# Score pass of a graph-attention kernel: three of four tiles as three rounded products, masks from ScalarE's signs

## What is computed

```
node_support = adj_n @ h
edge_output  = gru_cell(node_support, h, edge weights)
for each of 3 heads:
    hW = h @ W[k]
    hp = (adj_n > 0) @ hW ;  hm = (adj_n < 0) @ hW
    e_plus  = leaky_relu([hp, hm] @ a[k]) ; e_minus = leaky_relu([hm, hp] @ a[k])
    att = softmax over columns of (e_plus where adj_n > 0, e_minus where adj_n < 0, else -9e15)
    edge_support += (att * adj_n) @ hW / 3
node_output = gru_cell(edge_support, h, node weights)
x + diag(adj) * edge_output + diag(adj) * node_output
```

## Time and profile before

| what | value |
|---|---|
| median of the runs | 2155.43 us |
| the profiled execution | 2154.86 us, span 2153.1 us |
| TensorE busy | 89% of the span |
| VectorE, ScalarE busy | 77%, 58% |
| score pass, first table product to last f32 product | 922.0 to 1236.0 us |
| one of its chunks 1 to 7 | 39.8 us |

### The profile page before, as it was taken

The page is one execution under the profiler, slowest core; times in us unless marked ns, Lnnn a source line. Parts: engine busy times, 40 slices in busy tenths (PEclk is TensorE's granted clock), DMA queues, the critical chain, the costliest instruction groups (busy, mean ns, idle before and its releaser), DMA issues.

```text
span 2153.1 us, 21391 instructions
## 1 busy us (share of the span) xinstructions
PE 1910.1 (89%) x7805; PEld 1162.6 (54%) x7805; DVE 1652.7 (77%) x2442; ACT 1248.5 (58%) x1393; POOL 0.8 (0%) x7
## 2 busy tenths in 40 slices
PE   2336999699988889899999959899999999999997
PEld 1224888478878888844444436544444444444443
DVE  4668999698868989976656553498898888988985
ACT  3445666356669898810000010298878788887873
POOL 0000000000000000000000000000000000000000
PEclk9999999899999999999999979999999999999998
DMA  9999999488866767678998658632342323323220
GB/s 389 429 429 360 338 337 340 178 296 320 321 254 233 254 220 251 226 282 299 322 331 299 238 228 295 206 113 98 118 141 84 126 99 112 111 104 127 101 75 11
DMA packets 81561, 489.48 MB, mean 227 GB/s; under 512 B 8449, under 2 KB 12546, under 8 KB 36402
## 3 DMA queue, kind: packets, MB, share of 16 engines
q1 hardware_dynamic: 77138, 485.94, 61.7%
q10 hardware_dynamic: 4320, 2.20, 0.3%
HBM read 452.36 MB, written 35.75 MB: 227 GB/s over the span
## 4 chain that ended last, share of the span: by engine, by line
PE 70%; DVE 15%; DMA 7%; ACT 6%; issue 2%; SPq 0%; DVEq 0%; ACTq 0%
PE bank L1599 25%; PE bank L1483 10%; DMA ring<-in_adj_rows 6%; PE bank L1411 5%; PE bank L1413 5%; PE bank L1412 5%; PE bank L1561 5%; PE bank L1445 4%; DVE work L1255 3%; ACT work L573 2%; ACT work L566 2%; DVE a_lo L874 2%; PE bank L1478 2%; DVE reg L1255 1%; PE bank L1288 1%
## 5 line engine op out<-in xcount | busy, mean ns | idle before, releaser
L1599 PE MATMUL bank<-work,reg 128*128 128x512 f32 x960 | 423.0, 596 | 17.3 <-DVE ring L1204 11.4
L1255 DVE TENSOR_TENSOR work<-work,ring 128x1536 f32<-128x1536 f32 x160 | 280.2, 1752 | 68.4 <-ACT work L696 67.4
L1599 PEld LDWEIGHTS bank<-work,reg 128*128 128x128 f32 x960 | 182.0, 191 | 246.6 <-issue 220.3
L874 DVE TENSOR_TENSOR a_lo<-ring,a_hi 128x2048 fp32r<-128x2048 f32 x128 | 290.8, 2288 | 31.4 <-ACT a_hi L515 30.5
L515 ACT ACTIVATE a_hi<-ring 128x2048 fp32r<-128x2048 f32 x128 | 244.2, 1913 | 76.4 <-PE bank L1413 76.4
L1445 PE MATMUL bank<-reg,ring 128*128 128x129 f32 x2048 | 244.9, 281 | 36.9 <-DVE ring L988 36.8
L1445 PEld LDWEIGHTS bank<-reg,ring 128*128 128x128 f32 x2048 | 238.7, 197 | 42.4 <-DVE ring L988 32.5
L1599 PE MATMUL bank<-reg 128*128 128x512 f32 x576 | 252.4, 592 | 0.0
L696 ACT ACTIVATE work<-work 128x1536 f32<-128x1536 f32 x160 | 235.3, 1471 | 26.1 <-DVE work L1233 26.1
L1483 PE MATMUL bank<-ring,reg 128*128 128x512 f32 x512 | 236.8, 605 | 0.0
L1411 PE MATMUL bank<-a_hi,s_hi 128*128 128x512 f32 x512 | 207.0, 404 | 21.2 <-DVE a_lo L874 21.2
(11 more groups left out here) (214 smaller groups left out, 2153.5 us busy)
## 6 DMA issues: line engine op xcount, KB each, us to landing
ring<-in_adj_units SPq DMA_DIRECT2D x320, 1024.0 KB, 4.9
ring<-in_adj_rows SPq DMA_DIRECT2D x32, 2048.0 KB, 17.0
masks<-work SPq DMA_DIRECT2D x64, 512.0 KB, 9.0
ring<-masks SPq DMA_DIRECT2D x64, 512.0 KB, 4.5
reg<-lines SPq DMA_DIRECT2D x8, 768.0 KB, 10.1
ring<-lines SPq DMA_DIRECT2D x8, 768.0 KB, 8.0
out<-ring ACTq DMA_DIRECT2D x8, 256.0 KB, 2.3
gru<-in_cells SPq DMA_DIRECT2D x1, 768.0 KB
```

Of the source, the lines that this page charges most:

```text
L874: dve.tensor_tensor(a_lo[:, ring_at(p, g)], ring[:, ring_at(p, g)], a_hi[:, (g % 4) * UNIT:(g % 4 + 1) * UNIT].bitcast(F32), ALU.subtract) ...
L1255: dve.tensor_tensor(tv, tv, spread(ring[:, ring_at("out", g, q * W, W)], HEADS, 1), ALU.mult).then_inc(s_y, 1)
L1599: last = pe.matmul(bank[1 + k][:, :], h, tiles(c * T + t)[:, k * W:(k + 1) * W], start=t == 0, stop=t == T - 1)
```

## The change

In the score pass, of the four tiles of a unit, the first stays one f32 product (`WHOLE` = 1); the other three are made of three fp32r products each. For that ScalarE rounds 128x1536 values of each unit (`high_parts`, three buffers, `HIGHS`) and, in chunk 0, the 128x512 of `h` for that group; VectorE subtracts (`low_parts`). The masks are no longer compared on VectorE from f32 values: ScalarE writes the sign of the whole unit as fp8 (`sign_of`, 128x2048, two buffers in `hT` and `outT`), and VectorE makes the masks from its bits with two int32 operations over 128x512 words. A set mask is now 0.125, and the tables and sums are scaled for it. The steps of a chunk are at other places: on TensorE `turn_edge` behind unit `8c + 1`, `gates` behind `8c + 2`, `turn_cells` behind `8c + 7`; on VectorE and ScalarE as in the diff. Some buffers have moved (`sm_all`, `ucut`, `sums_sb`, the fourth mask buffer).

```diff
+    def sign_of(n):                                   # ScalarE
+        act.wait_ge(*loaded("edge", c, g))
+        if c == g: act.wait_ge(s_fix["edge"], g + 1)
+        if n > 1:  act.wait_ge(s_made, n - 1)
...
+        act.activation(signs[n % 2].bitcast(FP8), ring[:, ring_at("edge", g, c=c)],
+                       ACT.Sign, saturate=False).then_inc(s_sign, 1)
+    def high_parts(n):
...
+        if c == 0:
+            act.wait_ge(s_hkept, g + 1)
+            act.activation(h_hi[:, g * W:(g + 1) * W], reg1[:, g * W:(g + 1) * W], ACT.Copy).then_inc(s_hhi, 1)
+        if n >= HIGHS:
+            act.wait_ge(s_mm["edge"], n - HIGHS + 1)
+        act.activation(edge_hi(n), ring[:, ring_at("edge", g, WHOLE * W, SPLIT, c=c)], ACT.Copy).then_inc(s_ehi, 1)
+    for c in range(C):
+        for g in range(G):
+            n = c * G + g
+            if n == 3:             store_hT(C)
+            if c and g == 2:       keep_edge(c)
+            if c and g == 5:       gates("edge", c)
+            if 2 <= n + 1 < C * G: high_parts(n + 1)
+            if c and g == 6:       candidate("edge", c)
+            if n + 2 < C * G:      sign_of(n + 2)
     def masks(n):                                     # VectorE
         if n >= MASKS:
             dve.wait_ge(s_mm["edge"], n - MASKS + 1)
             dve.wait_ge(s_stored[b], 16 * (n // MASKS))
-        dve.tensor_scalar(made[b][0], src, 0.0, None, ALU.is_gt, saturate=False)
-        dve.tensor_scalar(made[b][1], src, 0.0, None, ALU.is_lt, saturate=False).then_inc(s_mask, 1)
+        dve.wait_ge(s_sign, n + 1)
+        dve.tensor_scalar(minus, code, 2, NONZERO, ALU.logical_shift_right, ALU.bitwise_and).then_inc(s_neg, 1)
+        dve.wait_ge(s_neg, n + 1)
+        dve.scalar_tensor_tensor(plus, code, NONZERO, minus, ALU.bitwise_and, ALU.bitwise_xor).then_inc(s_made, 1)
+    def low_parts(n):
...
+        dve.wait_ge(s_ehi, n + 1)
+        dve.tensor_tensor(a_lo[:, rest], ring[:, rest], edge_hi(n).bitcast(F32), ALU.subtract).then_inc(s_elo, 1)
     for c in range(C):
         for g in range(G):
-            if 4 <= c * G + g + 1 < C * G: masks(c * G + g + 1)
-            if c and g == 0: edge_nodes(c)
-            if c and g == 2: cell_in("edge", c, s)
-            if c and g == 3: cell_end("edge", c, s)
-            if c and g == 5: result("edge", c)
+            if n == 6:             gat_project(C)
+            if c > 1 and g == 2:   result("edge", c - 1)
+            if c and g == 4:       edge_nodes(c)
+            if c and g == 6:       cell_in("edge", c, s)
+            if 2 <= n + 1 < C * G: low_parts(n + 1)
+            if c and g == 7:       cell_end("edge", c, s)
+            if n + 2 < C * G:      masks(n + 2)
+            clear(n + 3)
     def edge_unit(n):                                 # TensorE
         for q in range(Q):
-            last = pe.matmul(nacc, reg1[tile], ring[part])
+            if q < WHOLE: pe.matmul(nacc, reg1[tile], ring[part]); continue
+            if q == WHOLE: pe.wait_ge(s_elo, n + 1)
+            pe.matmul(nacc, h_hi[tile], hi)
+            pe.matmul(nacc, h_hi[tile], a_lo[part])
+            last = pe.matmul(nacc, h_lo[tile], hi)
...
-            if c and g == 0: turn_edge(c)
-            if c and g == 1: gates("edge", c)
-            if c and g == 4: turn_cells("edge", c)
+            if c and g == 1: turn_edge(c)
+            if c and g == 2: gates("edge", c)
+            if c and g == 7: turn_cells("edge", c)
```

More of the change, by code:

```diff
@@ L25 @@
 EPS = 1e-5
+NONZERO = 0x20202020
+MASK_VALUE = 0.125
 SLOPE = 0.2
@@ L188, in gat_acc @@
             return bank[b][:, (i % 2) * 256:(i % 2) * 256 + P + 1]
-        SP = 7168
+        SP = 7680
         sp_all = work[:, SP:SP + T * EPAD // 2].bitcast(BF16)
-        sm_all = work[:, SP + T * EPAD // 2:SP + T * EPAD].bitcast(BF16)
-        ucut = work[:, 6144:6144 + 2 * Q * SCORES]
+        sm_all = reg4[:, N:N + T * EPAD // 2].bitcast(BF16)
+        ucut = gd[:, 0:2 * Q * SCORES]
         def plus_minus(region, b):
@@ L199, in plus_minus, with edge_hi @@
             return both[:, 0:UNIT // 4].bitcast(FP8), both[:, UNIT // 4:UNIT // 2].bitcast(FP8), both.bitcast(FP8)
-        made = [plus_minus(work, b) for b in range(MASKS)]
-        sums_sb = work[:, 4096:4096 + W]
         temps = ring[:, RING_EDGE * UNIT:G * UNIT]
         e_temps = [temps[:, i * W:(i + 1) * W] for i in range(6)]
+        made = [plus_minus(work, b) for b in range(MASKS - 1)] + [plus_minus(temps, 3)]
+        sums_sb = hn[:, :]
+        signs = [b[:, 0:UNIT // 4] for b in (hT, outT)]
+        SPLIT = (Q - WHOLE) * W
+        def edge_hi(n):
+            first = (MASKS - 1) * UNIT // 2 + (n % HIGHS) * SPLIT
+            return a_hi[:, first:first + SPLIT]
         kept = [plus_minus(ring[:, RING_OUT * UNIT:G * UNIT], b) for b in range(MLOADS)]
@@ L606, in candidate @@
                 act.activation(gn, gt, ACT.Tanh).then_inc(s_ga[p], 1)
[L608 to L611, removed]
+            for c in range(C):
+                for g in range(G):
+                    n = c * G + g
+                    if n == 3:
+                        store_hT(C)
+                    if c and g == 2:
+                        keep_edge(c)
+                    if c and g == 5:
+                        gates("edge", c)
+                    if 2 <= n + 1 < C * G:
+                        high_parts(n + 1)
+                    if c and g == 6:
+                        candidate("edge", c)
+                    if n + 2 < C * G:
+                        sign_of(n + 2)
             keep_edge(C)
@@ L997, in clear_diagonal, with clear @@
                 dve.wait_ge(s_fix[p], g + 1)
+            def clear(n):
+                c, g = n // G, n % G
+                if n < C * G and c == g:
+                    dve.wait_ge(*loaded("edge", c, g))
+                    clear_diagonal("edge", g)
             def masks(n):
[L1001 to L1004, removed]
+                b = n % MASKS
                 if n >= MASKS:
@@ L1057, in result @@
                 last.then_inc(s_res[p], 1)
+            clear(0)
             masks(0)
@@ L1062, in _ @@
             gat_nodes_in(C, s)
-            masks(2)
             gat_project(C - 1)
+            low_parts(0)
             gat_nodes_out(C, s)
-            masks(3)
-            gat_project(C)
+            low_parts(1)
             for c in range(C):
@@ L1071, in _ @@
                 for g in range(G):
-                    if 4 <= c * G + g + 1 < C * G:
-                        masks(c * G + g + 1)
-                    if c and g == 0:
+                    n = c * G + g
+                    if n == 6:
+                        gat_project(C)
+                    if c > 1 and g == 2:
+                        result("edge", c - 1)
+                    if c and g == 4:
                         edge_nodes(c)
-                    if c and g == 2:
+                    if c and g == 6:
                         cell_in("edge", c, s)
-                    if c and g == 3:
+                    if 2 <= n + 1 < C * G:
+                        low_parts(n + 1)
+                    if c and g == 7:
                         cell_end("edge", c, s)
-                    if c and g == 5:
-                        result("edge", c)
+                    if n + 2 < C * G:
+                        masks(n + 2)
+                    clear(n + 3)
+            result("edge", C - 1)
             edge_nodes(C)
```

81 lines of the change are left out of this document (64 added, 17 removed).

## The result

The changed kernel took 2171.68 us, the median of four runs (2170.12 to 2172.74), beside 2154.44 us for the kernel before (four runs): a ratio of 1.0079, with a 95% interval of 1.0067 to 1.0091. It is slower, by 17.2 us; 2165 was forecast. The profiled execution took 2170.12 us, with a span of 2168.3.

The account below looks back on a forecast made before the run. TensorE was taken to bound the score pass. Start +5.3, cheaper products -28.8 and seven waits of 4.7 us sum to +9.4 us, so 2165 us from the median of 2155.4; 8-in-10 range 2145 to 2181.

Parts of the forecast that it names:

- The wait: Score pass, TensorE: gates stands still for edge_nodes, queued behind masks(8c + 5), 4.7 us in each of seven chunks.
- The holder: VectorE in a chunk: masks(8c + 5) waits for unit 8c + 1's store to land, so gates stalls L - 5.7 us.
- the lower bound of 1.0 us by ScalarE's chain: If stores weren't late: high parts, sign, masks and edge_nodes end at +9.1 us, still stalling gates 1.0 us.
- L: Time from issue to landing of a mask store in the score pass, taken as 10.4 us, upper bound 13.
- rival C: DMA becomes the bound: loads pile up, stores land in 13 us, +27.6, 2183 us; chance 0.12 together with D.
- The clock: TensorE's granted clock in the score pass: a fall was costed at nothing, but listed as a sign of being wrong.
- The saving on TensorE: Three fp32r products replace an f32 one in three tiles: 0.51 us a unit, -28.8 us over chunks 1 to 7.
- The start: Chunks 0 and 1: late low parts and ScalarE's 4.0 us a unit cost +3.5, a held sign +1.8, together +5.3.
- The operations: Durations on ScalarE and VectorE: sign 1.91 us, high part 1.47, int32 step 0.42, low part 1.75; no table load.
- A: Stores land in 6.7 us or less, ScalarE's chain alone stalls gates 1.0 us: -16.5, 2139 us; chance 0.24 with its flank.
- B: A wash: stores land in 8.6 to 9.5 us, stall 2.9 to 3.8, 2152 to 2159 us; chance 0.16.
- D: VectorE's int32 operation at 0.69 us and a table load in each chunk's chain: +1.9 and up to +9.0 on top.

Follow-up runs that it names:

- moved_only: The kernel before with only the steps of a chunk moved to the change's places, f32 products and VectorE comparisons kept: 2203.38 us, ratio 1.0221.
- stores_ahead: The changed kernel with the store of unit n + 1's masks issued ahead of the load of unit n + 6: 2160.36 us, ratio 1.0031.
- nodes_early: The changed kernel with edge_nodes in VectorE's slot 2 of a chunk instead of slot 4: 2130.69 us, ratio 0.9892.

## Why the prediction was right, and where its terms were off

**The wait.** Right in kind and place: `gates` waits in each chunk for an `edge_nodes` that stands behind the masks of unit `8c + 5`, and one edit to that place turns the loss into a gain. Its size was wrong: "in each chunk 4.7" (L = 10.4) was 3.4 in the mean, 23.6 for seven chunks instead of 32.9.

**The holder.** Half right for the change itself. "`masks(8c + 5)` needs the landed store" is what happens with the old masks (76.5 us of waits of VectorE in `moved_only`), and in chunks 6 and 7 of the changed kernel. In chunks 1, 2, 3 and 5 ScalarE's sign comes later than the store. The step that failed there is the lower bound of 1.0 us by ScalarE's chain: "`high_parts(8c + 4)` starts when unit `8c + 1` is done". It took ScalarE as free at that point. In chunks 6 and 7 it was: the high parts began 0.2 us behind the start of `turn_edge` and the sign ended 3.5 behind it, where the prediction's terms give 3.4. In chunk 2 it wasn't. `turn_edge` behind unit 17 starts at 1011.90, so these high parts could have begun there; they began at 1014.79, 2.9 us late, since the sign of the diagonal unit had been held for 2.63 us and `keep_edge`'s 1.2 us were ahead in ScalarE's queue. With that the bound by ScalarE was about 3.9 us, not 1.0, and that is why removing one of the two brought little. The prediction's hold of a sign by `clear` was counted in chunk 1 alone; it comes once in each of the chunks 1 to 6.

**The landing time.** L was taken from the worst row, 10.4, since 430 GB/s between the gates seemed more than the DMA engines give. The seven stores that matter landed in 7.4 to 9.7 us, 8.5 in the mean. The rate of the changed kernel's pass in 40 equal slices, of 7.3 us each, shows that they come near it:

```profile
GB/s 393 392 423 114 103 397 377 416 381 46 228 408 389 421 273 27 364 373 421 404 135 159 381 408 425 349 10 366 372 417 397 161 104 400 379 408 403 98 74 0
```

In between the queue runs dry (slices of 46, 27 and 10), so it drains in every stall. The mask stores landed in 8.3 us median, 9.7 at most, over 957 to 1250 us: not over the old median of 9.0, and far from rival C's 13. The Trainium skill (DMA: Bandwidth & Descriptors, Specifications) gives about 358 GB/s as a core's share of the memory and 435 as the fabric's ceiling; the estimate beside rival C (2188 us) rested on the first. The slices of up to 425 are over the first and stay under the second, in a program on one core.

**The clock.** This term was missing; the prediction "has it at nothing", and named it as something that would make it wrong. Each gate product is two records, a pair. From the start of a chunk's first pair to its fifth it is 5.20 us behind a wait (1020.31 to 1025.51, and the same within 0.02 in the six chunks 2 to 7), and 3.51 in `stores_ahead` where the clock stays up (1138.87 to 1142.38). So such a wait costs 1.7 us more than itself, at 1.2 instead of 2.4 GHz. In chunk 1 it is 5.93 us (978.01 to 983.94), 2.4 more. Together 2.4 + 6 x 1.7 = 12.6 us. Filling the waits shortened the pass by 9.9: its 15 products are 24.0 us, 0.4 more than the waits had been, and 2.9 us of waiting were left. `stores_ahead` fits as well: behind two of its waits (2.51 and 1.12 us) the clock stays up, and its chunk 1 has 5.21, so 2 x 1.7 + 0.7 = 4.1 us of clock come to the 4.5 us of waiting, 8.6 in all.

**The saving on TensorE.** Right, a little too large. 28.8 us were forecast for chunks 1 to 7. A chunk without a wait is 35.88 us by two starts of `turn_edge` in `nodes_early` (1110.57 and 1146.45; 35.7 forecast), so the saving is 7 x 3.9 = 27.3; two units without a step between them start 3.69 apart (3.66 forecast). The 29.4 of the table are another sum: they have the units of chunk 0 in them.

**The start.** The size was too large. From the pass's first table product to that of unit 8 it is 38.06 us, 35.24 in the kernel before: +2.8, where +3.5 was forecast.

```profile
923.73 0.40 PE L1566 MATMUL bank<-work 128*32 128x512 fp8e4 x4
...
961.79 0.40 PE L1566 MATMUL bank<-work 128*32 128x512 fp8e4 x4
```

The forecast had 4.0 us a unit in chunk 0, the sum of ScalarE's three durations. But its operations start before the one ahead has ended by the profile: two starts of high parts are 3.70 apart, level with TensorE's 3.69. Against that stands the clock: unit 0 began its rounded products at 930.34, at half clock. For chunk 1 another +1.8 was forecast; without a wait of `gates` it is 36.2 us in `nodes_early`, +0.3. Together +3.1 instead of +5.3. (The 5.7 of the table are close to 5.3 by chance: there chunk 0 has f32 products.)

**The operations.** All right: the sign took 1.897 us (1.91 taken), a high part 1.476, the int32 step 0.424 (0.42), a low part 1.755. No table load comes with Sign: the pass has one at `gates`' first Tanh, as before. The Trainium skill (ScalarE: Activation LUTs, table sets) doesn't name Sign among the functions of every set; this trace shows it without a load of its own beside Copy and Tanh.

**The sum.** The forecast was +5.3 - 28.8 + 32.9 = +9.4. The two profiled executions differ by 15.3: +3.1 for the start, -27.3 for the products, +23.6 for the waits, +12.6 for the clock behind them, and +1.7 that is there already when the pass begins (923.73 beside 922.03), behind passes that the change doesn't touch; 1.6 stay unexplained. What the late place costs is seen between two marks, `turn_edge(1)` and the reductions behind the pass, in the changed kernel and in `nodes_early`:

```profile
969.09 0.98 PE L1589 MATMUL bank<-select,hn 128*128 128x19 f32 x8
...
1253.24 0.41 DVE L1174 TENSOR_REDUCE top<-e 128x3 f32<-128x192 f32 x1
```

```profile
966.85 1.07 PE L1589 MATMUL bank<-select,hn 128*128 128x19 f32 x8
...
1213.41 0.41 DVE L1174 TENSOR_REDUCE top<-e 128x3 f32<-128x192 f32 x1
```

Between them lie 284.2 and 246.6 us: 37.6 more, of which 23.6 are waits and 12.6 the clock, which leaves 1.4. The other 2.2 us are already there at `turn_edge(1)`, and already at the pass's first table product (923.73 beside 921.58), so the edit hasn't made them; whether another execution would show them stays open. The forecast came as near to the measured time as it did by luck: waits 9.3 us too long and a start 2.2 too dear stand against a clock of 12.6 left out and a saving 1.5 too large. The range of 2145 to 2181 held the time, the forecast's own range of 2158 to 2176 as well; rivals A, B and C are out, and so is D, as every operation had its duration and no table load came with the chain.

## What to carry to other kernels

A small step that a bottleneck engine will wait for is best placed in the first slot of its engine where its input is there; two slots too late cost 41 us here, more than the 29 that cheaper products brought. When a new wait is bounded by several chains, follow each of them through its engine's whole queue, with what holds that engine before, and not in one chunk alone: a unit with extra work, here the one with the diagonal, can change which chain is last. When the second is right behind the first, a fix to either alone shows little, and a fix to the place shows all. Price a wait of some microseconds on TensorE with the products behind it at half the clock as well.

## What the runs showed of the hardware beyond that

The clock's loss isn't in proportion to the wait. In the eight kernels here whose `gates` wait, the pairs behind the 16 waits of up to 1.58 us were at full clock, each time; behind the seven of 2.04 to 2.51 us four times not, and from 2.71 us on never. From 2.07 to 3.34 us of waiting, where there was a loss, it was 1.5 to 1.7 us; from 3.6 to 5.2 us it was 1.5 to 3.1. Near the lower end two almost equal waits went apart. In the changed kernel `gates` waited 2.48 us, and the clock was halved from the second pair on: the first starts 0.93 before it, the next ones are 1.68 and 1.70 apart. In `stores_ahead` it waited 2.51 us, and no two pairs were more than 0.93 apart. The first two pairs of the changed kernel and of `stores_ahead` (the second pair takes 1.88 us in the one, 1.02 in the other):

```profile
1142.37 1.11 PE L1602 MATMUL bank<-ring,gru 128*128 128x512 f32 x2 [2.48 <-DVE e L1104]
1143.30 1.88 PE L1603 MATMUL bank<-reg,gru 128*128 128x512 f32 x2
```

```profile
1138.87 1.10 PE L1604 MATMUL bank<-ring,gru 128*128 128x512 f32 x2 [2.51 <-DVE e L1106]
1139.80 1.02 PE L1605 MATMUL bank<-reg,gru 128*128 128x512 f32 x2
```

Products that nobody reads, put into the waits, made this kernel 13.7 us faster by the medians, 9.9 of them in the pass. That is a repair for a wait that can't be moved; here it could be.
